# Function sets of ScalarE loaded by hand, a sigmoid computed as an exponential, and a new merge table, in a fused two-block kernel

## What is computed

```python
# block 0, mixer (a selective scan; d_inner 512, d_state 16)
gate = silu(xn @ W_gate);  z = xn @ W_in
dt = clip(softplus(z @ W_dt + b_dt), 0.001, 1.0)
h  = exp(dt_t * A) * h + dt_t * B_t * z_t          # over 2048 steps
y  = einsum('bds,bs->bd', h, C_t) * gate;  out = x + y @ W_out
# block 0, feed-forward: one expert of 8 behind a softmax
probs = softmax(xf @ Wr.T)
y = (gelu(xf @ W1[7] + b1[7]) @ W2[7] + b2[7]) * probs[:, 7:8]
# block 1, mixer: a scan with a decay
beta = sigmoid(x @ Wbeta + b_beta)
# block 1, feed-forward: attention-like part and three experts chosen by bids
att = sigmoid(xln @ Wr) * (xln @ Wv) @ Wo
confidences = sigmoid(h @ conf);  difficulty = sigmoid(h @ w_diff)
bids = confidences * capital_shares * difficulty + affinity
winners = argmax(bids)
experts 0, 1: square(relu(h @ K)) @ V;  expert 2: (h @ W1 * sigmoid(state @ W2)) @ W3
```

## Time and profile before

| | |
|---|---|
| median of 3 runs | 3269.24 us (3268.8 to 3269.72) |
| profiled execution | 3268.99 us, span 3267.0 us |
| PE busy | 2928.0 us (90%) |
| DVE busy | 2684.9 us (82%) |
| ACT busy | 2109.7 us (65%) |
| POOL busy | 1969.2 us (60%) |
| a full chunk | about 188.5 us, chunks 2 to 15 alike |
| after the last scan | 238 us |
| mean granted TensorE clock | 0.93 |

### The profile page before, as it was taken

The page is one execution under the profiler, slowest core; times in us unless marked ns, Lnnn a source line. Parts: engine busy times, 40 slices in busy tenths (PEclk is TensorE's granted clock), DMA queues, the critical chain, the costliest instruction groups (busy, mean ns, idle before and its releaser), DMA issues.

```text
span 3267.0 us, 45469 instructions
## 1 busy us (share of the span) xinstructions
PE 2928.0 (90%) x14848; PEld 2392.1 (73%) x14848; DVE 2684.9 (82%) x4436; ACT 2109.7 (65%) x3852; POOL 1969.2 (60%) x1701
## 2 busy tenths in 40 slices
PE   7576799998999999899999999899999989999898
PEld 4355577787877778687777778777777878777776
DVE  3968989797988979798898979799897979989441
ACT  3555486776758676675767667675866767585443
POOL 1857667475766757565776756566675756666110
PEclk8577699999999999999999999999999999999998
DMA  4241132231422232232313233131332323133122
GB/s 130 82 163 58 50 109 69 98 114 65 141 78 97 76 111 97 87 122 69 110 62 117 91 112 107 65 112 67 111 101 98 107 73 123 59 104 118 46 89 90
DMA packets 152787, 308.56 MB, mean 94 GB/s; under 512 B 18372, under 2 KB 96988, under 8 KB 135144
## 3 DMA queue, kind: packets, MB, share of 16 engines
q1 hardware_dynamic: 152008, 302.52, 27.7%
q0 software_dynamic: 272, 1.57, 0.1%
q10 hardware_dynamic: 272, 1.57, 0.1%
HBM read 288.27 MB, written 17.35 MB: 94 GB/s over the span
## 4 chain that ended last, share of the span: by engine, by line
PE 31%; DVE 28%; issue 18%; ACT 14%; POOL 4%; DMA 2%; DVEq 1%; POOLq 0%; SPq 0%; ACTq 0%
DVE acc L1495 12%; DVE hs L1531 10%; PE ps_B L1771 8%; PE ps_A L1771 7%; PE ps_H L1766 4%; PE ps_H L1784 4%; PE ps_B L1766 3%; ACT ps_A L1302 2%; POOL bu L1151 2%; PE ps_B L1924 2%; PE ps_B L1784 2%; PE ps_B L1876 2%; DVE hA L1725 2%; DMA ws_in<-w_split 1%; ACT nn L727 1%
## 5 line engine op out<-in xcount | busy, mean ns | idle before, releaser
L1151 POOL TENSOR_TENSOR bu<-z,bb 128x512 f32<-128x512 f32 x1024 | 1294.5, 1285 | 344.5 <-DVE hs L1531 286.5
L1531 DVE TENSOR_TENSOR_SCAN hs<-ps_A,state,bu 128x512 f32<-128x512 f32 x768 | 976.1, 1276 | 26.4 <-ACT ps_A L1302 12.9
L1302 ACT ACTIVATE ps_A<-dt,a_neg 128x512 f32<-128x512 f32 x1024 | 700.1, 687 | 450.4 <-DVE hs L1531 448.5
L1766 PE MATMUL ps_H<-ident,hs 128*128 128x128 f32 x4096 | 653.4, 295 | 203.3 <-DVE acc L1495 113.5
L1766 PEld LDWEIGHTS ps_H<-ident,hs 128*128 128x128 f32 x4096 | 522.6, 152 | 348.6 <-DVE acc L1495 151.5
L1495 DVE SCALAR_TENSOR_TENSOR acc<-ps_H,ctok,acc 128x512 f32<-128x512 f32 x960 | 699.5, 730 | 32.7 <-PE ps_H L1766 31.9
L1876 PE MATMUL ps_B<-ws_out,hid 128*128 128x256 f32 x2944 | 694.8, 381 | 2.4 <-ACT hid L1354 2.2
L1876 PEld LDWEIGHTS ps_B<-ws_out,hid 128*128 128x128 f32 x2944 | 535.7, 191 | 66.6 <-ACT hid L1354 2.6
L1771 PE MATMUL ps_B<-fh,ws_in 128*128 128x512 f32 x1440 | 534.8, 417 | 9.2 <-DMA ws_in<-w_split 4.6
L1771 PEld LDWEIGHTS ps_B<-fh,ws_in 128*128 128x128 f32 x1440 | 270.7, 188 | 68.1 <-DVE bl L1686 7.9
L1531 DVE TENSOR_TENSOR_SCAN hs<-ps_A,bu 128x512 f32<-128x512 f32 x256 | 310.5, 1215 | 10.5 <-POOL bu L1151 6.0
(11 more groups left out here) (351 smaller groups left out, 4806.8 us busy)
## 6 DMA issues: line engine op xcount, KB each, us to landing
ws_in<-w_split SPq DMA_DIRECT2D x126, 1024.0 KB, 6.3
bb<-b_rows SPq DMA_DIRECT2D x256, 256.0 KB, 3.6
ws_out<-in_L_ffn_V_rwkv SPq DMA_DIRECT2D x64, 512.0 KB, 5.3
ws_out<-in_L_ffn_W SPq DMA_DIRECT2D x32, 512.0 KB, 8.1
xb<-in_L_attn_x SPq DMA_DIRECT2D x16, 512.0 KB, 6.3
n<-in_L_attn_x SPq DMA_DIRECT2D x16, 512.0 KB, 4.1
w_split<-wsp SPq DMA_DIRECT2D x8, 1024.0 KB, 5.6
out<-xb SPq DMA_DIRECT2D x16, 512.0 KB, 3.0
```

Source lines behind the costliest of these rows:

```text
L1151: pool.tensor_tensor(bu[:, u % 4, :], z[:, d, :], bb[:, s % 2, :], ALU.mult)\
L1302: act.activation(b.t[:, :], dt[:, d, :], ACT.Exp, scale=a_neg[:, d, s:s + 1])\
L1531: dve.tensor_tensor_scan(hs[:, s % 2, d, :], b.t[:, :], bu[:, k % 4, :], state[:, s, d:d + 1] if i % CPB else 0.0, ALU.mult, ALU.add)\
L1766: return pe.transpose(dst, src, ident[:, :])
```

## The change

It has three parts.

1. **Loads by hand.** A helper `load_table` emits the load of a set given by name. It is called at four places a chunk: ahead of the waits of `gate0` (Silu), of `softplus0` (the set with exponential and logarithm), of `gelu0`, and right behind `gelu1` (the set with exponential and Tanh). The load itself waits for nothing.
2. **Bids.** The Sigmoid of `sg` becomes an exponential of the negated logits on ACT, and DVE adds one and takes the reciprocal: two more steps at the head of `choice` (`OWN["dve_x"]` from 46 to 48).
3. **Merge table.** All five engines' numbers in `PACE` are new.

```diff
+TABLES = {"exp tanh": 0, "exp ln": 6, "gelu": 10, "silu": 18}
...
 PACE = {
     "sp": {
-        "w_in4": 73, "w_out3": 79, "w_in5": 82, "w_out4": 85, "w_in6": 87, "w_out5": 87, "w_in7": 91, "w_out6": 91,
+        "w_in4": 64, "w_out3": 73, "w_in5": 73, "w_out4": 83, "w_in6": 84, "w_out5": 87, "w_in7": 87, "w_out6": 96,
...
+        def load_table(act, functions):
+            act.add_instruction(mybir.InstLoadActFuncSet(name=nc.get_next_instruction_name(), engine=act.engine,
+                                                         act_func_set_id=TABLES[functions]))
...
                         yield f"gate{k}"
+                        if k == 0:
+                            load_table(act, "silu")
...
                         yield f"softplus{k}"
+                        if k == 0:
+                            load_table(act, "exp ln")
                         act.wait_ge(s_clip.sem, s_clip.at(i, k + 1))
...
                         yield f"gelu{h}"
+                        if h == 0:
+                            load_table(act, "gelu")
...
                         act.activation(blocks, blocks, ACT.Gelu).then_inc(f_gelu.sem, 1)
+                        if h == 1:
+                            load_table(act, "exp tanh")
...
-                    act.activation(X.sg[:, :, :], X.bl[:, :, 0:4], ACT.Sigmoid).then_inc(X.x_sg.sem, 1)
+                    act.activation(X.sg[:, :, :], X.bl[:, :, 0:4], ACT.Exp, scale=-1.0).then_inc(X.x_sg.sem, 1)
...
                     dve.wait_ge(X.x_sg.sem, X.x_sg.at(j, 1))
+                    own_step(dve.tensor_scalar(X.sg[:, :, :], X.sg[:, :, :], 1.0, None, ALU.add))
+                    own_step(dve.reciprocal(X.sg[:, :, :], X.sg[:, :, :]))
...
-OWN = {"pool_n": 5, "dve_f": 7, "dve_x": 46}
+OWN = {"pool_n": 5, "dve_f": 7, "dve_x": 48}
```

More of the change, by code:

```diff
@@ L168 @@
     "sp": {
[8 rows of a table removed]
-        "last_out": 380,
[8 rows of a table added]
+        "last_out": 375,
     },
     "pool": {
[L180 to L185, removed]
+        "w_low0": 38, "w_low1": 55, "w_low2": 61, "w_low3": 67, "w_low4": 85, "w_low5": 88, "w_low6": 119, "w_low7":
+        120, "mean0": -40, "rstd0": -29, "h0": -21, "mean1": -15, "rstd1": 5, "gx": 24, "u0": 25, "u1": 25, "u2": 25,
+        "u3": 25, "xg": 44, "rstd_a": 113, "x_prob": 163, "end_rstd_a": 107, "end_x_prob": 145, "rstd_e": 198, "h2":
+        198, "x_bias": 198, "rstd_h": 214, "rstd_i": 218, "rstd_j": 218, "rstd_m": 239, "x5": 289, "last_rstd_e": 167,
+        "last_h2": 167, "last_x_bias": 168, "last_rstd_h": 170, "last_rstd_i": 182, "last_rstd_j": 189, "last_rstd_m":
+        189, "last_x5": 272,
     },
     "act": {
[18 rows of a table removed]
[18 rows of a table added]
     },
     "dve": {
[6 rows of a table removed]
[6 rows of a table added]
         231, "att0": 234, "att1": 235, "m_stats": 235, "lowh0": 241, "lowh1": 241, "bids": 244, "tw0": 245, "tw1":
         245, "choice": 245, "tr": 247, "e0": 263, "e1": 279, "x5": 279, "last_e_stats": 151, "last_kq0": 151,
[6 rows of a table removed]
[6 rows of a table added]
     },
     "pe": {
[7 rows of a table removed]
[7 rows of a table added]
         "end_d7": 145, "h2T0": 185, "h2T1": 185, "kq0": 186, "kq1": 187, "kq2": 189, "kq3": 189, "kvT0": 191, "kvT1":
[1 row of a table removed]
[1 row of a table added]
         "r0": 228, "v0": 229, "r1": 231, "v1": 231, "sW0": 232, "sW1": 232, "att0": 234, "att1": 234, "hhT0": 239,
[15 rows of a table removed]
[15 rows of a table added]
     },
```

## The result

| | before | changed |
|---|---|---|
| median | 3269.02 us (3267.75 to 3269.72) | 3240.92 us (3240.63 to 3243.26) |
| ratio | | 0.9916, 95% interval 0.9899 to 0.9933 |
| profiled span | 3267.0 us | 3238.8 us |
| busy PE, DVE, ACT, POOL | 2928.0, 2684.9, 2109.7, 1969.2 us | 2921.7, 2693.9, 2069.2, 1947.0 us |
| granted clock, mean | 0.931 | 0.943 |

The changed kernel is 28 us faster, 0.84%. The forecast was 3249 us in a range of 3228 to 3272: the sign and the place were right, the gain was 28 us where 20 were forecast.

What follows compares the result with a forecast made beforehand. It took the front's chain over ACT and POOL to DVE's scans, then a full DVE, as the bound. A full chunk: -1.7 + 0.4 = -1.3 us; fourteen -18.2, chunks 0 and 1 -2: 3249 us, range 3228 to 3272.

Steps and rivals of the forecast that it cites:

- the place: Front of each chunk, ACT's chain through POOL to DVE's scans: ninth scan 1.7 us earlier, full chunk 1.3 us shorter.

Runs made afterwards that it cites:

- after_tanh: Changed kernel with the bids' sigmoid as Tanh of half the argument, its 1 and halves taken into existing DVE steps; 3233.8 us, ratio 0.9899.
- after_sigmoid: Changed kernel with Sigmoid for the bids again, without the two DVE steps, two loads a chunk more; 3234.8 us, ratio 0.9904.
- after_lexp_load: Changed kernel with one load more a chunk, of the set at hand, ahead of the router's exponential; 3241.5 us, ratio 0.9924.
- rows_only: Kernel before with two merge table numbers changed (ACT, PE), so that `rows_f` stands ahead of its pair of `fh`; 3278.1 us, ratio 1.0026.
- after_rows_back: Changed kernel with one number of ACT's table changed, so that `rows_f` stands behind its pair of `fh` again; 3256.2 us, ratio 0.9971.
- after_rv_back: Changed kernel with weight slot `rv` behind the third row `bb` in SP's queue again; 3254.6 us, ratio 0.9957.
- loads_only: Kernel before with the four calls of `load_table`, nothing else; 3259.0 us, ratio 0.9988.

## What to carry to other kernels

Don't count loads of a function set; ask at each one who waits for the activation behind it: twenty-nine fewer were worth nothing (after_tanh against after_sigmoid), and one a chunk that ran beside a wait instead of behind it was worth 7 us. An engine that is on no chain of the stage can still be in it by its clock: a PE that idles 2.4 us and then runs at half speed delays a small transpose, and with it everything that stands behind its consumer in another queue. And price a move of an order in the order that it will stand in: one and the same move of `rows_f` was worth 15 us in one table and cost 8 us in the other.

## What the runs showed of the hardware

- After waits of 2.3 to 2.4 us for `rows_f` the granted clock fell in 8 to 12 of 14 chunks. After waits of 0.8 to 1.0 us it fell at this place in none of 14, in seven executions; in one of them (after_lexp_load) a wait of 1.55 us followed 5.7 us later, without a fall either. In rows_only, where one of 2.1 us followed 6.3 us later, it fell behind that one in three. In one and the same execution (after_rows_back), with the same wait of 2.3 to 2.4 us in each chunk, it fell in eight chunks and not in six; what decides between them stays open.
- The length of a wait alone does not tell: in after_rv_back the clock fell in four of 14 chunks behind a wait for weights of 0.9 to 1.9 us, with shorter waits of PE just ahead of it (0.58 and 0.60 us in one of them), and in ten behind like waits it did not.
- Like executions differ by the clock of their last stage: 0.91 and 238.2 us in the trace of before, 0.96 and 231.0 us in that of loads_only, with the same 910 matmuls.
- A transfer of 256 KB issued 2.9 us behind one of 1 MB landed 3.0 to 3.7 us later, ahead of POOL's need for it at 4.9 us. Issued 0.6 to 0.9 us behind one (four chunks of after_rows_back) it took 4.5 to 4.9 us. Issued 0.4 us ahead of it (after_rv_back), both came late: PE waited 0.97 us, and the ninth scan moved 0.4 us.
- A load of a function set took 1.283 us in each case, whether the set was at hand already (after_lexp_load) or not.
